# One-hot comparison of a recommendation kernel: ids shifted once, both tables of a pair compared at a time

## What is computed

```python
e = jnp.stack([tbl_0[ids[:, 0]], tbl_1[ids[:, 1]], ..., tbl_26[ids[:, 26]]], axis=1)
interactions = jnp.einsum('bfd,bgd->bfg', e, e).reshape(B, F * F)
z = jnp.concatenate([bottom, interactions[:, TRIL_IDX]], axis=1)
h = jnp.concatenate([z, bottom], axis=1)
h = jnp.maximum(h @ W_top1 + b_top1, 0.0)      # 607 -> 512
h = jnp.maximum(h @ W_top2 + b_top2, 0.0)      # 512 -> 256
y = h @ W_top3                                 # 256 -> 1
```

## Time and profile before

| what | us |
|---|---|
| median of three runs | 432.13 |
| lowest and highest run | 430.05, 432.84 |
| the profiled execution, its time | 432.13 |
| the profiled execution, its span in the profile | 430.3 |
| TensorE busy (matmuls) | 390.4 |
| VectorE busy | 273.7 |
| ScalarE busy | 168.9 |
| GpSimd busy | 290.1 |
| the 640 compares of line 436 on VectorE | 195.0 |
| the 1280 matmuls of line 748 on TensorE | 181.9 |
| the 272 gathers of line 400 on GpSimd | 289.3 |

### The profile page before, as it was taken

How to read it: one execution, slowest core, us unless ns; L and a number is a source line. 1 busy time by engine, 2 the same in 40 slices (tenths; PEclk the granted TensorE clock), 3 DMA queues, 4 the chain that set the end, 5 groups by cost and what they waited for, 6 DMA issues and landing times.

```text
span 430.3 us, 9369 instructions
## 1 busy us (share of the span) xinstructions
PE 390.4 (91%) x3222; PEld 369.5 (86%) x3222; DVE 273.7 (64%) x806; ACT 168.9 (39%) x338; POOL 290.1 (67%) x279
## 2 busy tenths in 40 slices
PE   0586889969999899999999899998999899999987
PEld 0575789959998899989998899988998899989976
DVE  4888438974479446884479446883479446874241
ACT  2243342344522363235522463225522463235544
POOL 6787778777877778777887778777787778600000
PEclk9968899998999999999999999999999999999999
DMA  5999933454135551444234751548244551720000
GB/s 112 239 230 235 257 102 85 96 97 135 45 110 103 101 131 37 138 95 139 63 99 96 101 130 39 138 88 138 68 100 99 104 130 41 134 45 3 2 2 0
DMA packets 49791, 44.20 MB, mean 103 GB/s; under 512 B 30309, under 2 KB 42093, under 8 KB 49767
## 3 DMA queue, kind: packets, MB, share of 16 engines
q1 hardware_dynamic: 39440, 24.26, 28.7%
q0 software_dynamic: 8704, 17.84, 15.3%
q10 hardware_dynamic: 1623, 1.79, 1.8%
HBM read 39.01 MB, written 4.85 MB: 102 GB/s over the span
## 4 chain that ended last, share of the span: by engine, by line
PE 82%; SPq 5%; DVE 4%; ACT 4%; DMA 3%; issue 2%; ACTq 0%
PE ps_build L748 34%; PE ps_gram L779 21%; PE ps_dense L787 14%; PE ps_gram L775 3%; SPq L301 3%; PE ps_build L758 3%; DVE hot L436 3%; DMA raw<-tbl_dram 3%; ACT embT L568 2%; PE ps_gram L758 2%; PE ps_dense L824 2%; PE ps_gram L787 1%; SPq L302 1%; ACT embT L561 1%; SPq L293 1%
## 5 line engine op out<-in xcount | busy, mean ns | idle before, releaser
L400 POOL DMA_INDIRECT rows<-tbl_dram,idx x272 | 289.3, 1064 | 84.5 <-issue 78.0
L748 PE MATMUL ps_build<-hot,table 125*128 125x256 f32 x1280 | 181.9, 297 | 23.7 <-DVE table L415 16.5
L436 DVE TENSOR_SCALAR hot<-id_raw,vocab 125x256 fp32r<-125x256 int32 x640 | 195.0, 377 | 8.4 <-DMA id_raw<-ids_onehot_dram 7.0
L748 PEld LDWEIGHTS ps_build<-hot,table 125*128 125x128 f32 x1280 | 166.0, 199 | 34.3 <-issue 15.9
L779 PE MATMUL ps_gram<-embT 128*107 128x104 f32 x896 | 92.7, 262 | 10.8 <-ACT embT L568 10.8
L779 PEld LDWEIGHTS ps_gram<-embT 128*107 128x107 f32 x896 | 88.7, 177 | 15.8 <-ACT embT L568 11.2
L561 ACT COPY embT<-ps_build 128x512 f32<-128x512 f32 x40 | 32.0, 801 | 123.1 <-PE ps_build L748 109.3
L450 DVE COPY gram<-ps_gram 107x416 f32<-107x416 f32 x56 | 32.9, 587 | 54.1 <-PE ps_gram L779 54.0
L580 ACT COPY gram<-ps_gram 107x416 f32<-107x416 f32 x56 | 28.4, 507 | 58.1 <-PE ps_gram L779 58.1
L415 DVE TENSOR_TENSOR h<-ps_dense,h 128x256 fp32r<-128x256 f32 x28 | 11.9, 425 | 41.1 <-ACT h L602 40.8
L787 PE MATMUL ps_dense<-pairT,w1p 120*128 120x256 f32 (+1 forms) x252 | 34.8, 283 | 0.0
(11 more groups left out here) (65 smaller groups left out, 190.5 us busy)
## 6 DMA issues: line engine op xcount, KB each, us to landing
id_raw<-ids_onehot_dram SPq DMA_DIRECT2D x40, 256.0 KB, 5.9
gram_dram<-gram SPq DMA_DIRECT2D x56, 84.5 KB
raw<-tbl_dram SPq DMA_DIRECT2D x10, 448.0 KB
rows<-tbl_dram,idx POOLq DMA_INDIRECT x272
bot<-bottom_dram SPq DMA_DIRECT2D x8, 128.0 KB, 5.6
w1p_raw<-w_pairs_dram ACTq DMA_DIRECT2D x1, 720.0 KB
raw<-tbl_dram SPq DMA_DIRECT2D x10, 52.0 KB
w_raw<-w_dram ACTq DMA_DIRECT2D x1, 512.0 KB
```

Of the source, the lines that this page charges most:

```text
L400: nc.gpsimd.indirect_dma_start(rows[:, t, s * D:(s + 1) * D], None, tables[f], bass.IndirectOffsetOnAxis(idx[:, 2 * i + t, f:f + 1], 0)).t ...
L436: last = nc.vector.tensor_scalar(hot[0:VP, a % HOT_SLOTS, v, :], id_raw[0:VP, n % ID_SLOTS, q, :], vocab[0:VP, row:row + 1], None, ALU.is_ ...
L748: last = nc.tensor.matmul(bank[:, q * HALF:(q + 1) * HALF], table[0:VP, units[n][q], bits, row:row + D], hot[0:VP, a % HOT_SLOTS, v, :], s ...
```

## The change

The ids of a unit, both tables at once, are turned into fp32 less `vocab[p, 0]` = 8p, in place in their slot of `id_raw`, by one subtraction over 2 x 256 elements with a per-partition operand. The compares wait for it on a semaphore of its own (`id_shifted`). A compare then takes the shifted ids of both tables, 512 elements, and an instruction constant, the number v, in place of the per-partition operand. A part is now two rows v of both tables (`VS`), so it is two compares and still 8 matmuls, and a unit still has four parts. `hot` keeps its size. TensorE goes through a part by table, then row v, then high and low; in half 0 it waits for the low parts of both tables ahead of a unit. Only the first matmul of a unit starts the bank.

```diff
-    parts = [(n, q, v0) for n, unit in enumerate(units) for q in range(len(unit)) for v0 in range(2)]
+    VS = 2
+    parts = [(n, v0) for n in range(len(units)) for v0 in range(0, VB, VS)]
...
-        hot = sb("hot", [128, HOT_SLOTS, VB // 2, HALF], fp32r)
+        hot = sb("hot", [128, HOT_SLOTS, VS, 2, HALF], fp32r)
...
             def make_hot(i, a):
-                n, q, v0 = parts[a]
-                if q == v0 == 0:
+                n, v0 = parts[a]
+                w = len(units[n])
+                shifted = id_raw[0:VP, n % ID_SLOTS, 0:w, :].bitcast(fp32)
+                if v0 == 0:
                     s = n % ID_SLOTS
                     per_half = len(range(s, len(units), ID_SLOTS))
                     dve.wait_ge(id_in[s], 16 * (per_half * i + n // ID_SLOTS + 1))
+                    nc.vector.tensor_scalar(shifted, id_raw[0:VP, n % ID_SLOTS, 0:w, :], vocab[0:VP, 0:1], None,
+                                            ALU.subtract).then_inc(id_shifted, 1)
+                    dve.wait_ge(id_shifted, len(units) * i + n + 1)
...
-                for v in range(VB // 2):
-                    row = v0 * VB // 2 + v
-                    last = nc.vector.tensor_scalar(hot[0:VP, a % HOT_SLOTS, v, :], id_raw[0:VP, n % ID_SLOTS, q, :],
-                                                   vocab[0:VP, row:row + 1], None, ALU.is_equal)
+                for v in range(VS):
+                    last = nc.vector.tensor_scalar(hot[0:VP, a % HOT_SLOTS, v, 0:w, :], shifted, float(v0 + v), None,
+                                                   ALU.is_equal)
                 last.then_inc(hot_made, 1)
...
                 for a in parts_of(n):
-                    _, q, v0 = parts[a]
+                    v0 = parts[a][1]
                     if is_half(i, FIRST) and v0 == 0:
-                        pe.wait_ge(table_low, units[n][q] + 1)
+                        pe.wait_ge(table_low, units[n][-1] + 1)
                     pe.wait_ge(hot_made, HOTS * i + a + 1)
-                    for v in range(VB // 2):
-                        row = (v0 * VB // 2 + v) * D
-                        for bits in (HIGH, LOW):
-                            last = nc.tensor.matmul(bank[:, q * HALF:(q + 1) * HALF],
-                                                    table[0:VP, units[n][q], bits, row:row + D],
-                                                    hot[0:VP, a % HOT_SLOTS, v, :], start=(v0 == v == bits == 0),
-                                                    stop=(v0 == 1 and v == VB // 2 - 1 and bits == LOW))
+                    for q in range(len(units[n])):
+                        for v in range(VS):
+                            row = (v0 + v) * D
+                            for bits in (HIGH, LOW):
+                                last = nc.tensor.matmul(bank[:, q * HALF:(q + 1) * HALF],
+                                                        table[0:VP, units[n][q], bits, row:row + D],
+                                                        hot[0:VP, a % HOT_SLOTS, v, q, :],
+                                                        start=(v0 == v == q == bits == 0),
+                                                        stop=(v0 == VB - VS and v == VS - 1 and bits == LOW),
+                                                        skip_group_check=True)
                     last.then_inc(built if ends_unit(a) else hot_used, 1)
```

More of the change, by code:

```diff
@@ L237, in dlrm_tower @@
         dve_step = sem("dve_step")
+        id_shifted = sem("id_shifted")
         out_done = sem("out_done")
```

## The result

| what | before, us | after, us |
|---|---|---|
| median | 431.72 | 417.81 |
| lowest and highest run | 430.05, 432.84 | 416.00, 418.98 |
| the profiled execution, its time | 432.13 | 418.98 |
| its span | 430.3 | 417.2 |
| the compares on VectorE | 195.0 (640) | 120.0 (320) |

The ratio of the medians is 0.9677, with a 95% interval from 0.9629 to 0.9725: 3.2% faster. (The runs of before here are those taken beside the changed kernel.) Forecast were 417.6 us.

A forecast was written before the change was run, and what follows sets the result against it. VectorE's compares were taken to bound the build stage from unit 2 on. Span 430.3 - 14.0 (halves 1 to 6) - 0.7 (half 7) + 0.2 (half 0) = 415.8, plus 1.8 gives 417.6 us; range 414.5 to 426.5.

The forecast's parts named there:

- The limit and the stage: Build stage, VectorE-bound from unit 2: units from 5.00 to TensorE's 4.28 us, gain 2.33 us in halves 1-6, 0.73 in half 7.
- The compare: VectorE: two results a cycle; 512 elements cost 0.40 to 0.48 us, eight of them 3.2 to 3.8 us a unit.
- lower bound: Compare's fixed part on VectorE: 0.07 us, as other instructions have, against the 0.13 of the old compare; 0.34 us in all.
- 0.40 to 0.48 from start to start: Sign that the forecast is right: the spacing in us of 512-element compares on VectorE.
- just in time: Build stage: VectorE has part 7 at 273.5 us latest, needed at 273.9, and unit 2 at 275.1, needed at 275.34.
- The subtraction: VectorE, one per unit over 512 elements: 0.40 us, 0.51 with the wait of the next compare, up to 0.7 with GpSimd.
- GpSimd's share: Compares beside gathers on VectorE: 0.05 us on 0.263, 19%, taking the new compare from 0.40 to 0.48 us.
- Half 0: First half, tables arriving slowly: waiting for both tables of a unit loses 0.2 us in place of a gain.
- A: Build stage: VectorE still binds, 4.7 us a unit, as the subtraction's wait lets gathers in; 426 us, chance 10%.
- B: Gathers: GpSimd becomes the bound, each build-stage gather waiting 0.47 us more; 8 us lost, 426 us, chance 8%.
- C: VectorE: the new compare makes one result a cycle, 0.60 us each, 5.55 a unit; slower, 445 us, chance 8%.
- D: Build stage: no difference, an unseen wait keeps the 5.00 us a unit; 432 us, chance 4%.

The follow-up runs named there:

- constants alone: Kernel before plus the subtraction, 256-element compares with a constant, TensorE's old order: 419.41 us, ratio 0.9694; 608.45 and 613.68 us on the disturbed chips.
- experiment 6: Changed kernel, in half 0 weight loads issued between tile 0's emptyings and TensorE waiting for each table's low part separately: 418.79 us, ratio 0.9691 to before.
- experiment 3: Changed kernel with a third, unused 512-element compare in each part, 12 a unit: 4.72 us a unit; 596.49 and 601.47 us on disturbed chips.
- experiment 1: Changed kernel with compares added behind its last output, GpSimd idle: 256/512 elements 0.2625/0.396 us with per-partition operand, 0.202/0.3355 with constant.
- width alone: Changed kernel without its subtraction, 512-element compares on int32 ids with per-partition operand: 440.87 us, ratio 1.0187; 615.1 and 617.88 us on disturbed chips.

## Why the prediction was right, point by point

**The limit and the stage: right.** From the start of half 1's units to the end of the span took 430.3 - 69.08 = 361.2 us before and 417.2 - 70.55 = 346.7 after: gain 14.6, with 14.0 + 0.7 forecast. The stretch is 346.8 in the second profile of the change, 346.6 with constants alone and 346.8 in experiment 6. The stage behind kept its length (25.7 us from the last matmul of unit 4 to the next half's first, in both). What varies from run to run is half 0.

**The compare: right in kind, mis-sized within its bounds.** Two results a cycle was right (0.1335 us for 256 more elements). Taken were 0.40 us, with the row of the same operation for the fixed part; the constant form has the 0.07 of the lower bound, 0.336 alone and 0.344 to 0.356 beside gathers. So VectorE's unit is 3.3 us, not 4.1, and of the signs named for right, "0.40 to 0.48 from start to start" did not come. It cost nothing in the forecast, since both are under 4.28; what was "just in time" came 0.7 us early for part 7 (ready at 265.37, needed at 266.1) and 0.9 for unit 2.

**The subtraction: right.** Its start to the next compare is 265.88 - 265.37 = 0.51 us; 0.51 was forecast.

**GpSimd's share: half right.** It did not stay a fixed share of the compare's time. The compares now give little (0.344 to 0.356 for 0.336), and the gathers beside the dense stream take 0.94 to 1.19 us where nearly all took 0.945 before (one 1.11). But the long ones have shrunk: before had four of 1.63 to 2.14 us in each steady half, about the stretch where VectorE empties pair products and makes four compares at a time, and the one of 4.05; after has two of 1.31 to 1.55 there. So the mean fell from 1.064 to 1.037. At 109.30 us, 78 gathers were begun, for 76 in the earlier trace rows.

**Half 0: the term that missed.** Forecast was a loss of 0.2 us; against the one kept profile of before (69.08) the two profiles gave a loss of 1.47 and a gain of 1.65. Units 3 and 4 begin where forecast or somewhat earlier (39.23 and 47.07, for 39.6 and 47.4), so waiting for both tables was priced rightly. What the sum kept fixed is how long TensorE takes for a unit there. Unit 4 took 4.08 us in before, 5.56 in the first profile (1.2 GHz for its first 17 matmuls) and 4.07, from an earlier start at 45.48, in the second. Its last matmul ends at 51.27, 52.63 and 49.55, so 1.36 of the 1.47 lost and all of the 1.65 won lie there; the rest, some 0.1 us, is ScalarE's copies. The prediction had the slow unit in its range ("a slow one may turn out otherwise") and not in its sum. The end of half 0 scatters from 67.43 to 70.55 over six profiles (that of before among them), so no single profile can carry a step of 0.2 us there. In the sum the miss of 1.27 is nearly all of the 1.4 between the forecast span, 415.8, and 417.2.

**The number: closer than it could be known.** 417.6 was forecast and 417.81 measured, beside a kernel before that had moved from 432.13 to 431.72; the second series has 416.20 beside 433.46. With half 0 scattering by 3 us, an agreement within 0.2 is luck. What is confirmed is the gain from half 1 on, 14.6 us for 14.7, in both profiles of the change.

**Rivals.** A is excluded by the 4.28 us units. A VectorE that binds again at some 4.7 us a unit is what experiment 3 made, but with more compares and not by the wait on the subtraction. C is excluded by experiment 1, D by the result. B did not happen with this change, but it had been priced too cheaply as a danger: had the change widened the compares only, it would have been the outcome. For that kernel the same terms gave an expectation of 417 to 419 us, and it took 441. The argument put against B, that most gathers already lie beside compares and are near their minimum, doesn't hold for other forms of compare.

## What to carry to other kernels

When two engines are within a few per cent of each other in a stage, work out what each takes without the other: here VectorE's unit was 4.2 us alone, 5.0 beside GpSimd, and TensorE's 4.28, so any cut that clears the line is worth 0.7 us a unit and no more. In this kernel the instruction constant in place of a per-partition operand was the half of the change that paid alone; a wider compare with the operand kept also took VectorE under the line, yet held the gathers and handed the bound to GpSimd. Check the neighbour's budget for every form considered (gathers per half times their mean and the 0.30 us between them, against the half). Look at the single records behind an average: 0.313 us a compare was 0.26 three times and 0.47 once. And when the chain of waits goes through one engine, see when the others would have been ready: here ScalarE's long issues were within 0.1 us of TensorE. And don't draw a verdict on a form from a chip on which the kernel before itself does not run at its usual time.

## What the runs showed of the hardware

- A per-partition operand costs a VectorE compare 0.06 us over a constant, whatever its width (0.2625 to 0.202, 0.396 to 0.3355); int32 or fp32 input is the same.
- Which of VectorE and GpSimd gives depends on the form of the stream. Old compares (256, per-partition operand) in a long stream: 0.313 for 0.264, one in four delayed by 0.2 us and the others not at all, with gathers near 0.945; in short bursts it is the gathers that give, four of 1.63 to 2.14 us in a steady half, and one of 4.05. Wide ones with that operand, in a long stream: nothing given while a gather is held for up to 6.03 us. With constants, in streams of 8 to 16: 0.344 for 0.336 (512) and 0.22 for 0.202 (256), gathers to 1.2 us; beside short bursts gathers of 1.3 to 1.7. The Trainium skill, SBUF — State Buffer, section Who interferes with whom, has the shared port pair taken for the whole instruction by whoever issues first. The trace agrees that one of the two can be held for long, and differs in the rest: three compares in four keep their price while a gather is at work, and a gather was held over some 15 instructions on end (6.03 / 0.396). The spans of GpSimd in a profile are rough; why the forms differ stays open.
- TensorE's granted clock in half 0 differs between executions of the same kernel: unit 4's matmuls began at 0.52 (1.2 GHz) in one profile of the changed kernel and ran at 1.00 in the other, behind idle times of 1.85 and 1.80 us.
- On two chips TensorE, VectorE and ScalarE stood still together in stretches, and the kernel before took 639 and 644 us for 432; the stages in between had their usual lengths. GpSimd and the DMA engines went on for at least part of them: in width alone (`wide_int_b`) the three engines have no busy time from 268 to 276 us, GpSimd has six gathers there, and the DMA engines' busy share is 0.78 to 0.86. On the same chip the kernel with the gathers of half 0 alone took 442 us, and half 1 to the end went undisturbed. So the standstills go with the gathers; whether the gathers make them, or the traffic that they bring, was not tried.
